# Running a feed-forward stage inside the steps of a state-space stage, block by block

## Chip, cores and metric

The kernel runs on one core of a Trainium2 chip. The metric is the device time of one execution in microseconds, as the median of several. The engines are TensorE (PE, with its weight loads PEld), VectorE (DVE), ScalarE (ACT), GpSimd (POOL) and SyncE (SP), which here only issues DMAs. Each engine works through its own queue in the order in which the program writes it, and waits on semaphores for the others.

## What is computed

Four layers follow each other over x of 16 sequences x 256 tokens x 128 channels. A windowed attention, a mixture-of-experts layer with an attention of its own, a state-space layer (third stage) and a gated MLP (last stage). Only the last two matter here. In the reference's terms, for the third:

```python
xn = layernorm(x); u, z = split(xn @ W_in)
u = silu(causal_depthwise_conv(u, conv_w) + conv_b)
dt = softplus(u @ dt_w + dt_b); Bm, Cm = u @ B_w, u @ C_w
h_t = h_{t-1} * exp(dt_t * A) + (dt_t * u_t) Bm_t;  y_t = h_t . Cm_t
x = x + layernorm(x_n + ((y + u * D) * silu(z)) @ W_out)
```

and for the last, token by token, with ternary weights and scales s:

```python
xn = layernorm(x)
hid = silu(xn @ w1 * s1) * (xn @ w2 * s2)      # 512 wide, gate and up
hid = gelu(hid @ h1 * t1); hid = gelu(hid @ h2 * t2)
x = x + layernorm(hid @ w3 * s3)
```

## The kernel before

**Tiling.** The channels or the tokens lie on 128 partitions. The third stage takes one sequence of 256 tokens per step; the state is handed from chunk to chunk of 8 tokens, and from one half of a sequence to the next. The last stage takes blocks of 512 tokens (two sequences), two blocks ("lanes") per pass, four passes. x stays in SBUF as xB. The precise matmuls split each operand into a high and a low part (`product`, L1405): three matmuls, high x high, low x high, high x low. A hidden product of the last stage has four groups (m), each of four k blocks x 3 matmuls of 128x512; a gate product has two times three. The last product takes sixteen 128x128 matmuls in float32.

**Order.** All is written out by hand. Each engine has a function `step_c(n, have)` for the third stage, called for n = 0 to 18, which holds that engine's share of work on sequences n-3 to n+4: a software pipeline. `have(k)` says whether sequence n+k exists. After it comes `step_d` for the last stage, called for the four passes. The loops stand at the end of each engine's part, for TensorE as

```python
pairs(0)
for n in range(0, NB + 3):
    step_c(n, within(n))
    if n == NB - 1:
        step_d(-1, 0, within(-1, ITER_MLP))
for n in range(0, ITER_MLP + 1):
    step_d(n, 0, within(n, ITER_MLP))
```

`step_d(-1)` norms and turns the first two blocks inside step 15.

**A step of the third stage.** TensorE: B and C inputs (`in_and_out`), step size (`step_size`), turning the next input (`turned_input`), outputs from states (`from_states`), C by chunk (`outputs_by_chunk`), the convolution as four shifted matmuls and z's matmul (`convolved`), the chunks' weights turned (`chunk_weights`), B by chunk (`inputs_by_chunk`), states (`chunk_states`), output product (`projected`), products of token pairs (`pairs`), turned states (`turned_states`). VectorE (L1300): the conv input, seven decay products (L1194), from states (L1203), terms (L1215, L1218: decay x pair products), adding (L1227), dt (L1239), masked C (L1244), gating (L1233), the scan (L1248), statistics, weighted input, states (L1270 to L1278), residual, masked B (L1288), the output norm's statistics. ScalarE (L852): Relu and Abs of dt (L764), the input turned (L781), Exp and Ln, skip path, `normed`, Silu of u and z (L812), two Exp for the decays (L818), output norm, states out, and B and C (L759). Its functions lie in different tables: Ln, Silu and Exp each load theirs, three loads a step. GpSimd: the pair sums (L546, L548), small norm arithmetic, products, and adding to xB (L560).

**A block of the last stage.** `gate` is Silu of the gate product (L901), `hid` the up product times scale and gate (L1347, "raised" in the change), h_h its high part (L892) and h_l its low part (L1340). Gelu after hidden product 1 is L909, with high part L910, and after hidden product 2 L914. The last product (L1843) is scaled on VectorE (L1374), normed (L109, L112, L118, L119, L141), added on GpSimd (L594) and stored by SyncE (L425).

**Buffers.** PSUM has eight banks. The third stage uses 0 to 3 for input, dt/C, B and state, 4 to 7 for the four groups of pair products, and 7 (2 for sequence 0) also for B and C. The last stage uses four banks per lane. The last stage's buffers lie over the third's in SBUF. The weights' high parts are made on ScalarE (L881, L884) and their low parts on GpSimd (L506), a quarter in step 14, the rest in the steps after 15.

## Time and profile before

| | |
|---|---|
| median of three runs | 1014.7 us |
| lowest and highest | 1014.23, 1015.83 us |
| profiled execution | 1014.94 us |
| its span | 1013.1 us |
| TensorE, VectorE, ScalarE, GpSimd busy | 84%, 67%, 55%, 44% |
| mean granted clock of TensorE | 0.85 |

The rows that follow come from one profiled execution. A row of a timeline gives start in us, duration in us, engine, line and operation, output <- input, shapes and count, and in brackets how long the engine had been idle and who released it. A window gives the busy time of each engine in a stretch. The granted clock is 1.00 at 2.4 GHz and 0.50 at 1.2 GHz; a value between is a mean over time. The stretch from about 500 to 720 us is the third stage, that from 731 us on the last.

### The profile page before, as it was taken

The numbers are of one execution on the slowest core, as the hardware profiler recorded it, in microseconds if no ns is written. First come the engines' busy times: TensorE is split into PE (matmuls) and PEld (weight loads), VectorE is DVE, ScalarE is ACT, GpSimd is POOL, SyncE is SP. The second block draws the span as 40 slices with busy tenths as digits, with TensorE's granted clock in tenths as the row PEclk, the third lists the DMA queues.
The fourth block names the chain that finished last, engine by engine and source line by source line (L and its number), as shares of the span: only waits on it lengthen the run. The fifth ranks groups of instructions, "written<-read, shape, count | busy, mean of one in ns | idle before, by whom it ended". The sixth has DMA issues, their size and how long they took to land. (4 is left out here: it accounts for less than half of the span.)

```text
span 1013.1 us, 21506 instructions
## 1 busy us (share of the span) xinstructions
PE 849.9 (84%) x8256; PEld 700.1 (69%) x8256; DVE 678.9 (67%) x1965; ACT 555.2 (55%) x1050; POOL 448.3 (44%) x765
## 2 busy tenths in 40 slices
PE   4887836789999999898587798887579999999994
PEld 4777735678888888676455576655468878888783
DVE  3888954757888878742499999999772180551712
ACT  3454523347666666546477877877354362542630
POOL 1676752314555554544477777866650020020201
PEclk9877865559999989887788977788589999999997
DMA  8300002000000000000000000000000000000000
GB/s 273 101 24 12 24 27 65 17 1 2 2 2 2 2 3 2 1 2 1 1 1 0 1 1 1 2 1 0 1 1 1 1 21 1 1 22 1 16 6 21
DMA packets 22149, 16.76 MB, mean 17 GB/s; under 512 B 2576, under 2 KB 20376, under 8 KB 21792
## 3 DMA queue, kind: packets, MB, share of 16 engines
q1 hardware_dynamic: 21040, 14.77, 4.7%
q8 instruction: 65, 1.06, 0.4%
q10 hardware_dynamic: 1008, 0.63, 0.2%
q14 instruction: 36, 0.29, 0.1%
HBM read 11.20 MB, written 4.19 MB: 15 GB/s over the span
## 5 line engine op out<-in xcount | busy, mean ns | idle before, releaser
L118 POOL TENSOR_TENSOR d_ln_ve<-d_ln_mv,eps 128x4 f32<-128x4 f32 x16 | 3.2, 201 | 228.3 <-DVE d_ln_mv L112 228.3
L1408 PE MATMUL ps<-h_h,wh_l 128*128 128x512 f32 x256 | 99.6, 389 | 0.0
L1409 PE MATMUL ps<-h_l,wh_h 128*128 128x512 f32 x256 | 99.6, 389 | 0.0
L1407 PE MATMUL ps<-h_h,wh_h 128*128 128x512 f32 x256 | 99.6, 389 | 0.0
L1486 PE MATMUL ps<-w_e,he 128*128 128x128 f32 x512 | 87.4, 310 | 3.7 <-ACT he L679 3.3
L679 ACT ACTIVATE he<-ps,pp 128x256 f32<-128x256 f32 x128 | 59.6, 471 | 43.9 <-PE ps L1409 39.2
L1486 PEld LDWEIGHTS ps<-w_e,he 128*128 128x128 f32 x512 | 77.2, 222 | 6.1 <-ACT he L679 5.4
L1420 PEld LDWEIGHTS ps<-mov,hbd 32*128 32x128 f32 x2048 | 75.1, 224 | 0.0
L1374 DVE TENSOR_TENSOR d_y<-ps,w_s 128x512 f32<-128x512 f32 x8 | 5.5, 692 | 103.0 <-PE ps L1843 103.0
L1420 PE MATMUL ps<-mov,hbd 32*128 32x32 f32 (+1 forms) x2048 | 74.0, 300 | 0.0
L1340 DVE TENSOR_TENSOR h_l<-hid,h_h 128x512 fp32r<-128x512 f32 x64 | 48.5, 772 | 31.2 <-ACT h_h L910 30.3
L118 POOL TENSOR_TENSOR b_ln_ve<-b_ln_mv,eps 128x2 f32<-128x2 f32 x64 | 13.1, 204 | 111.4 <-DVE b_ln_mv L112 111.4
L914 ACT ACTIVATE hid<-ps,pp 128x512 f32<-128x512 f32 x32 | 22.1, 690 | 62.3 <-PE ps L1409 62.3
L1407 PEld LDWEIGHTS ps<-h_h,wh_h 128*128 128x128 f32 x256 | 48.1, 188 | 10.1
L1409 PEld LDWEIGHTS ps<-h_l,wh_h 128*128 128x128 f32 x256 | 48.1, 188 | 10.0
L1408 PEld LDWEIGHTS ps<-h_h,wh_l 128*128 128x128 f32 x256 | 48.1, 188 | 9.9
L653 ACT ACTIVATE tau<-ps 128x768 f32<-128x768 f32 x32 | 24.2, 809 | 55.6 <-PE ps L1420 55.6
L1407 PE MATMUL ps<-hTh,we_h 128*128 128x256 f32 x128 | 53.6, 419 | 0.0
L1194 DVE TENSOR_TENSOR wall<-dec,wall 128x224 f32<-128x224 f32 (+6 forms) x112 | 47.8, 427 | 3.7 <-issue 0.3
L546 POOL TENSOR_TENSOR term<-term 128x224 f32<-128x224 f32 (+2 forms) x48 | 35.4, 737 | 32.4 <-DVE term L1218 29.9
L119 POOL TENSOR_TENSOR b_ln_rs<-b_ln_ve,half 128x2 f32<-128x2 f32 x64 | 46.0, 718 | 5.0
L1764 PE MATMUL ps<-ident,hc 128*128 128x128 f32 x64 | 15.0, 371 | 37.9 <-DVE hc L1278 37.9
(287 smaller groups left out, 2597.8 us busy)
## 6 DMA issues: line engine op xcount, KB each, us to landing
x<-in_x SPq DMA_DIRECT2D x16, 128.0 KB
w_h<-in_w_h SPq DMA_DIRECT2D x2, 1024.0 KB, 7.9
x<-x SPq DMA_DIRECT2D x16, 128.0 KB, 1.8
xB<-x SPq DMA_DIRECT2D x32, 64.0 KB
out_x<-xB SPq DMA_DIRECT2D x32, 64.0 KB
w_m<-in_w_m SPq DMA_DIRECT2D x3, 256.0 KB, 3.8
xB<-in_w_e SPq DMA_DIRECT2D x1, 512.0 KB
w_e<-in_w_e SPq DMA_DIRECT2D x1, 512.0 KB
```

The lines of the kernel that those rows point to most:

```text
L119: pool.tensor_tensor(self.rs[l][:, :], self.ve[l][:, :], half[:, 0:self.k], ALU.pow).then_inc(self.rstd_ready, 1)
L546: chain.link(pool.tensor_tensor(y[:, :, j:CH], y[:, :, j:CH], wide[:, HALF - 1 - j, :, j:CH], ALU.add))
L653: act.activation(tau[l][:, 2 * k:2 * k + 2, :], ps[:, 4 * l + 2 * k:4 * l + 2 * k + 2, 0:NBLK * SPAN], ACT.Sigmoid, scale=ATT_SCALE).then_ ...
L679: act.activation(he[e % 2][:, :], ps[:, HE + e % 2, 0:NT], ACT.Gelu, bias=vec("b1", e)).then_inc(he_ready, 1)
L914: act.activation(hid[l][:, m, :], bank(l, m), ACT.Gelu, scale=vec("h2_s", m)).then_inc(m_h2, 1)
L1194: ins = dve.tensor_tensor(wall[l][:, :, CH - 1 - j, j:CH], dec[l][:, 0, :, j:CH], wall[l][:, :, CH - j, j - 1:CH - 1], ALU.mult)
L1340: dve.tensor_tensor(dst[l][:, m, :], hid[l][:, m, :], high_part[l][:, m, :].bitcast(F32), ALU.subtract).then_inc(done, 1)
L1407: pe.matmul(dst, a_h, b_h, start=start, stop=True, skip_group_check=True)
L1408: pe.matmul(dst, a_l, b_h, start=False, stop=True, skip_group_check=True)
L1409: return pe.matmul(dst, a_h, b_l, start=False, stop=True, skip_group_check=True)
L1420: return pe.matmul(dst, hbd[l][heads(g), j, :, :].rearrange("p h s -> p (h s)"), mov[l][heads(g), BLK * j:BLK * j + w], start=False, stop= ...
L1486: last = pe.matmul(ps[:, ACC, P * c:P * c + P], he[e % 2][:, P * c:P * c + P], w_e2[:, e, :], start=False, stop=True, skip_group_check=True)
```

## The change

Blocks of 512 tokens of the last stage run inside the third stage's steps. Let b be a block: sequences 2b and 2b+1. In step n = 2b+4 ("entering") its tokens are normed and turned and gate products 0 and 1 are made; in step 2b+5 ("middle") gate products 2 and 3 and hidden product 1; in step 2b+6 ("ending") hidden product 2 and the last product; in step 2b+7 ("leaving") the output norm and the addition to xB. So an odd step has a middle block, an even one an ending and an entering one. The steps now run from 0 to 16 only. What is left after step 16, the rest of block 6 and all of block 7 but its place in memory, stands in a `tail()` on each engine, with PSUM banks of its own (`TAIL_UP`, `TAIL_HIDDEN`).

To make room, the last stage has one lane: a single `hid`, `h0`, `h1`, `d_xn`, `d_xh`, `d_y` and two `gate` and two `raw` buffers, some of them over the raw weights' memory. In PSUM the pair products get two banks (4, 5) and are made in two halves, `pairs(t, 0)` and `pairs(t, 1)`, with `terms` in two halves as well; the second half of `pairs` stands behind the convolution. Banks 6 and 7 are the last stage's; its last product goes to bank 2. The weights are split in ten parts, two in each of steps 0 to 4. The output norm of the third stage writes in place and comes a step earlier. TensorE's new `step_c`, cut:

```diff
             def step_c(n, have):
+                entering, middle, ending = block_of(n, 4), block_of(n, 5), block_of(n, 6)
                 if have(1):
                     in_and_out(n + 1)
                     step_size(n + 1)
...
                     from_states(n - 1)
+                if ending is not None:
+                    hidden(ending, 1, 0)
                 if have(1):
                     outputs_by_chunk(n + 1)
+                if middle is not None:
+                    gate_and_up(middle, 2)
                 if have(2):
                     convolved(n + 2)
+                if middle is not None:
+                    if have(1):
+                        inputs_by_chunk(n + 1)
+                    gate_and_up(middle, 3)
+                if have(0):
+                    pairs(n, 1)
+                if ending is not None:
+                    hidden(ending, 1, 1)
                 if have(0):
                     chunk_weights(n)
-                if have(1):
+                if middle is None and have(1):
                     inputs_by_chunk(n + 1)
+                if ending is not None:
+                    hidden(ending, 1, 2)
                 if have(0):
                     chunk_states(n)
+                if middle is not None:
+                    if have(1):
+                        pairs(n + 1, 0)
+                    hidden(middle, 0, 0)
                 if have(-1):
                     projected(n - 1)
-                if have(1):
-                    pairs(n + 1)
+                if ending is not None:
+                    hidden(ending, 1, 3)
+                if entering is not None:
+                    tokens_turned(entering)
+                if middle is None and have(1):
+                    pairs(n + 1, 0)
+                if middle is not None:
+                    hidden(middle, 0, 1)
                 if have(0):
                     turned_states(n)
+                if middle is not None:
+                    hidden(middle, 0, 2)
+                    hidden(middle, 0, 3)
+                if entering is not None:
+                    gate_and_up(entering, 0)
+                if ending is not None:
+                    last_product(ending)
+                if entering is not None:
+                    gate_and_up(entering, 1)
```

The new functions on TensorE, with what they wait for:

```diff
+            def gate_and_up(b, m):
+                if m == 0:
...
+                    pe.wait_ge(S["d_xl"], b + 1)
...
+                elif b < LAST - 1 or b == LAST - 1 and m == 1:
+
+                    pe.wait_ge(m_raw, nth(b, m - 1))
...
+            def hidden(b, w, m):
+                src_h, src_l, ready, done = ((h0_h, h0_l, m_h0, m_h1_ps), (h1_h, h1_l, m_h1, m_h2_ps))[w]
+                if m == 0:
...
+                    pe.wait_ge(ready, nth(b, HID - 1))
+                elif m >= 2 and b < LAST - 1:
+
+                    pe.wait_ge((m_h1_high, m_h2)[w], nth(b, m - 2))
```

ScalarE's and VectorE's new `step_c`, as the order of their calls (what is new stands with its block):

```diff
             def step_c(n, have):          # ScalarE
...
                     log_part(n + 1)
                 if have(0):
                     skip_path(n)
+                if middle is not None:
+                    high0(middle, 1)
+                    gated(middle, 2)
+                if ending is not None:
+                    hidden2(ending, 0)
                 if have(2):
                     normed(n + 2)
+                if ending is not None:
+                    hidden2(ending, 1)
+                if middle is None and have(0):
                     chunk_weights(n)
+                if ending is not None:
+                    hidden2(ending, 2)
+                    hidden2(ending, 3)
+                if entering is not None:
+                    turned_tokens(entering)
                 if have(2):
                     silus(n + 2)
+                if middle is not None:
+                    high0(middle, 2)
+                    gated(middle, 3)
+                    if have(0):
+                        chunk_weights(n)
+                    high0(middle, 3)
+                if entering is not None:
+                    gated(entering, 0)
...
+                    gated(entering, 1)
                 if have(1):
                     decays(n + 1)
+                if entering is not None:
+                    high0(entering, 0)
+                if middle is not None:
+                    hidden1(middle, 0)
...
             def step_c(n, have):          # VectorE
+                if entering is not None:
+                    tokens_in(entering)
                 if have(2):
                     conv_input(n + 2)
+                if leaving is not None:
+                    tokens_out(leaving)
+                if middle is not None:
+                    raised(middle, 1)
+                if ending is not None:
+                    low1(ending, 2)
+                    low1(ending, 3)
                 if have(0):
                     decay_products(n)
                 if have(-1):
                     from_states(n - 1)
+                if middle is not None:
+                    low0(middle, 0)
+                    low0(middle, 1)
+                    raised(middle, 2)
+                if have(0):
+                    terms(n, 0)
+                if have(1):
+                    step_size(n + 1)
+                if entering is not None:
+                    tokens_normed(entering)
+                if have(1):
+                    outputs_by_chunk(n + 1)
+                if middle is not None:
+                    low0(middle, 2)
+                    if have(1):
+                        summed_steps(n + 1)
+                    raised(middle, 3)
+                if have(0):
+                    terms(n, 1)
+                if middle is not None:
+                    low0(middle, 3)
...
                 if have(-1):
                     add_sums(n - 1)
                     gated(n - 1)
                 if have(1):
                     weighted_input(n + 1)
+                if leaving is not None:
+                    output_normed(leaving)
...
+                if entering is not None:
+                    tokens_low(entering)
                 if have(4):
                     statistics(n + 4)
+                if entering is not None:
+                    raised(entering, 0)
...
+                if ending is not None:
+                    scaled(ending)
+                if middle is not None:
+                    low1(middle, 0)
+                    low1(middle, 1)
```

In the last of these, `raised` is the up product times scale and gate into `raw`, `low0` and `low1` are low parts, `scaled` is the scaling of the last product, `tokens_in` and `tokens_out` are statistics, `tokens_normed` and `output_normed` apply norms. On ScalarE `high0` is the copy to the high part, `hidden1` Gelu with its copy, `hidden2` Gelu alone. SyncE's loop over the blocks is written out, with the same four stores a block.

## Rows read from the trace of the kernel before

**Rows 1.** The page: busy time of each engine; TensorE's granted clock in 40 slices.

```profile
PE 849.9 (84%) x8256; PEld 700.1 (69%) x8256; DVE 678.9 (67%) x1965; ACT 555.2 (55%) x1050; POOL 448.3 (44%) x765
...
PEclk9877865559999989887788977788589999999997
```

**Rows 2.** Windows: stretch, busy PE, PEld, DVE, ACT, POOL (x), clock, DMA.

```profile
550.00:600.00 50.00, 39.56 (x242) 29.34 (x240) 47.59 (x117) 39.00 (x80) 38.43 (x78) 0.82 0.00 1
...
800.00:850.00 50.00, 48.49 (x234) 40.14 (x233) 28.83 (x76) 26.35 (x39) 7.30 (x10) 1.00 0.04 11
```

**Rows 3.** One line: min/median/max ns, first, last start; one per step.

```profile
L1276 DVE TENSOR_TENSOR hc<-hd,ps x16: 420/420/422, 512.4 to 718.2; 128x256 f32<-128x256 f32 x16
```

**Rows 4.** Timeline, VectorE, last stage: start, duration, engine, line, [idle <-releaser].

```profile
800.35 0.69 DVE L1374 TENSOR_TENSOR d_y<-ps,w_s 128x512 f32<-128x512 f32 x1 [23.32 <-PE ps L1843]
...
994.66 0.69 DVE L1374 TENSOR_TENSOR d_y<-ps,w_s 128x512 f32<-128x512 f32 x1 [23.32 <-PE ps L1843]
```

**Rows 5.** Timeline, TensorE, third stage: one step.

```profile
596.88 0.75 PE L1764 MATMUL ps<-ident,hc 128*128 128x128 f32 x4 [1.28 <-DVE hc L1278]
...
606.62 0.93 PE L1757 MATMUL ps<-prod,ones 32*128 32x384 f32 x8
```

**Rows 6.** Timeline, TensorE, last stage: gate, hidden and last products.

```profile
816.35 0.40 PE L1407 MATMUL ps<-d_xh,wm_h 128*128 128x512 f32 x1
...
817.74 0.39 PE L1407 MATMUL ps<-h_h,wh_h 128*128 128x512 f32 x1
...
820.46 0.39 PE L1407 MATMUL ps<-h_h,wh_h 128*128 128x512 f32 x1
...
990.82 7.30 PE L1843 MATMUL ps<-w_m,hid 128*128 128x128 f32 x64
```

**Rows 7.** Timeline, ScalarE, third stage; the last row is Exp between Gelu calls.

```profile
595.07 1.28 ACT L818 ACT_TABLE_LOAD   x1
...
597.18 0.86 ACT L133 ACTIVATE c_o<-c_r,c_ln_nm,c_ln_rs 128x128 f32<-128x128 f32 x2
...
598.89 0.47 ACT L764 ACTIVATE c_zb<-ps,pp 128x256 f32<-128x256 f32 x1 [0.21 <-PE ps L1678]
...
602.95 0.86 ACT L798 ACTIVATE c_xn<-xB,c_ln_nm,c_rs 128x128 f32<-128x128 f32 x2
...
460.27 1.28 ACT L716 ACT_TABLE_LOAD   x1
```

**Rows 8.** Timeline, VectorE, third stage.

```profile
616.12 1.21 DVE L1215 TENSOR_TENSOR term<-wall,ps 128x1024 f32<-128x1024 f32 x1
...
617.85 0.41 DVE L1227 TENSOR_TENSOR c_yi<-c_yi,term 128x256 f32<-128x256 f32 x1
...
620.83 0.46 DVE L109 BATCH_NORM_STATS2 c_ln_st<-xB 128x6 f32<-128x128 f32 x2
```

**Rows 9.** Timeline, VectorE and ScalarE, last stage: element-wise operations.

```profile
817.28 0.75 DVE L1347 SCALAR_TENSOR_TENSOR hid<-ps,pp,gate 128x512 f32<-128x512 f32 x1 [1.10 <-ACT gate L901]
...
815.49 0.69 DVE L1340 TENSOR_TENSOR h_l<-hid,h_h 128x512 fp32r<-128x512 f32 x1
...
816.55 0.69 ACT L901 ACTIVATE gate<-ps,pp 128x512 f32<-128x512 f32 x1 [1.10 <-PE ps L1409]
...
832.27 0.63 ACT L910 ACTIVATE h_h<-hid 128x512 fp32r<-128x512 f32 x1
```

**Rows 10.** Windows, TensorE alone: one that is mostly idle, and the next.

```profile
524.58:528.00 3.42, 0.54 (x3) 0.90 0.00 0
...
528.00:531.41 3.41, 3.41 (x31) 0.60 0.03 7
```

**Rows 11.** One line: low parts of the last weights, GpSimd.

```profile
L506 POOL TENSOR_TENSOR wm_l<-w_m,wm_h x2: 1314/1338/1361, 709.7 to 711.0; 128x512 fp32r<-128x512 f32 x2
```

**Rows 12.** Timeline, TensorE, start of the last stage.

```profile
748.50 0.50 PE L1407 MATMUL ps<-d_xh,wm_h 128*128 128x512 f32 x1 [3.42 <-DVE hid L1347]
```

**Rows 13.** Timeline, end of the kernel: VectorE's scaling.

```profile
998.26 0.69 DVE L1374 TENSOR_TENSOR d_y<-ps,w_s 128x512 f32<-128x512 f32 x1 [2.91 <-PE ps L1843]
```

531 lines of the change are left out of this document (313 added, 218 removed).

## Prediction

> **What bounds the kernel now.** I read the page first. TensorE is busy 84% of the span, VectorE 67%, ScalarE 55%, and the granted clock is lowest where the third stage runs [rows 1]. A share over the whole span says little here, so the windows come next. They show two regimes. In the third stage VectorE is busy 47.6 of 50 us and TensorE 39.6 at a granted clock of 0.82; in the last stage TensorE is busy 48.5 of 50 us at 1.00, and VectorE only 28.8 [rows 2]. So the third stage hangs on VectorE's queue, the last on TensorE's, and work of the one could lie in the other's gaps. The rates: 16 steps of the third stage start one per (718.2 - 512.4)/15 = 13.72 us [rows 3]; three passes of the last stage take 994.66 - 800.35 = 194.3 us, 64.8 us for two blocks, 32.4 a block [rows 4]. Two steps and one block, which the change puts together, thus cost 27.4 + 32.4 = 59.8 us now.
>
> **What two steps and a block cost TensorE.** One step's operations run from 596.88 to 607.55, 10.7 us [rows 5], part of it at the half clock; at full clock I take 9.6. A gate product is 817.74 - 816.35 = 1.4 us, a group of a hidden product 820.46 - 817.74 = 2.72, the last products 7.30/2 = 3.6 [rows 6], turning the tokens 0.4 (estimate, four matmuls at 7.30/64). A block is 4 x 1.4 + 8 x 2.72 + 3.6 + 0.4 = 31.4. With two steps that is 50.6 us against 59.8. That is the least the pair can take, and 9 us of gain per pair the most.
>
> **What the order leaves of it.** The queues are written out by hand, so I walk them. An odd step has gate products 2 and 3 and hidden product 1 of the middle block, an even one hidden product 2 and the last products of the ending block and the first two gate products of the entering one. Time zero is the end of the even step's last products.
>
> (a) TensorE makes gate product 1, 1.4. ScalarE then has in its queue Silu 0.7 (and 0.14 to be released), a table load with two Exp, 597.18 - 595.07 = 2.1, a copy to the high part 0.6, the copy of bcT 0.3, then step size, turned input, Exp, table load, Ln and skip path, 602.95 - 598.89 = 4.1, a copy 0.6, and a table load with Silu 2.0: gate 2 is there at 11.8 [rows 6, 7, 9]. TensorE waits for parts of this: for the step size's Relu and Abs (about 1.7 us), and with gate product 3 for the raised gate 2 (about 1.8).
>
> (b) VectorE now has raised gate 2, both halves of terms, step size, masked outputs, the scan, two low parts and raised gate 3 ahead of the last low part of the hidden input. From terms to the scan's end it is 620.83 - 616.12 = 4.7, less 0.9 for adding and gating, which stay behind (the first takes 0.41), plus 0.1 for splitting terms in two; raised gates 0.75 and low parts 0.69 each, two of either: 6.7 us in all [rows 8, 9]. GpSimd waits for terms at that time, so that I take 0.6 off for operations that run longer beside it. Only then, at 18, may hidden product 1 begin. TensorE had waited another 2.2 us.
>
> (c) Four hidden groups 10.9, output product and turned states 1.2: 12.1. VectorE keeps ahead.
>
> (d) The even step on TensorE: 9.6 + 10.9 + 0.4 + 1.4 + 3.6 = 25.9, and 0.5 of waiting for the token's low part. ScalarE has five table loads there but reaches all of its releases in time by my walk, and VectorE has some 20 us of work in 27.
>
> The pair is 11.8 + 6.7 - 0.6 + 12.1 + 26.4 = 56.4 us.
>
> **The clock.** A mostly idle stretch (0.54 of 3.42 us busy) is followed by a slow phase of about 3.4 us, at 0.5, in all: 0.10 and 0.40 of two rows' clock is missing, twice that is the slow time [rows 10]. It costs 1.7 us if TensorE is what is waited for, nothing in front of a wait. The odd step's waits of 1.7, 1.8 and 2.2 us lie beside small matmuls, and before this change a wait of 1.28 us at 596 [rows 5] stood in a stretch with clock 0.82 [rows 2]. Bounds: 0, and 5.4 (three slow phases of which one falls on gate product 3, one on the first hidden group and one on the even step's first). I take one, 1.8: the first is absorbed by the wait after it. The pair is then 58.2 us, 1.6 under that of before.
>
> **The edits with a small price.** Pair products in two halves: the second half now stands behind the convolution, and it waits for the first half's terms. In steps 0 to 4 VectorE comes to the second half of terms about when TensorE has done the convolution at full clock, and up to 2 us earlier at half clock: bounds 0.1 and 2, I take 1.0 for five steps, 5.0. The weights' split goes from the boundary into steps 0 to 4. GpSimd gets 2 x 1.34 us a step [rows 11] on 10.5 of 13.7 (38.4 of 50 [rows 2]); it just fits (bounds 0 and 0.5 a step, in the 5.0). ScalarE gets 2 x 0.6; the last pair delays step 5 by 1.3. More table loads: 3 a pair, since Gelu comes into the steps and Exp after Gelu needs one, as in the second stage [rows 7]; they are in the walk. Output norm a step earlier and in place, the residual's wait for c_x, the shared bank of the last products: their releasers are over two steps old, nothing. SyncE's stores: the same four per block, earlier, under other work; the final ones have the same length behind them. Single buffers (raw, gate, d_y, banks 6 and 7): each wait's releaser comes in time by the walk, except those counted.
>
> **The sum**, in the profiled execution's own time. VectorE enters step 4 at about 556 (567.3 by rows 3, less the 11.5 us that stand ahead of that line in the step, estimate). Step 4 takes 13.9 and the tokens' statistics, norm, low part 3.0, plus gate product, Silu and raised gate behind it, less what covers them, 1.6: 574.2. With 5.0 and 1.3: 580.5. Five pairs 291.0: 871.5. Step 15 has no input to prepare: (a) shrinks to 8, 8 + 6.5 - 0.6 + 12.1 + 1.6 = 27.6: 899.1. Step 16: from states 1.6, hidden product 10.9, gate 1.4, last 3.6, small ones 1.0, waits 2.7: 21.2: 920.3. The tail: 1.4 gate product and 7.0 of waiting for gates 2 and 3 and their low parts; hidden groups 4 x 10.9; gates 5.6; last 7.2; turning with its wait 1.1; waits of 2.2 and 0.9 in front of the last block's two final products, which no second lane covers any more; end 12.7 (1013.1 - 998.3 [rows 13] and 0.2, less one block's norm, 2.3); one slow phase 1.7 and 0.6 more: 84.0. **The span is 1004.3.** What pays most is not the pair (5 x 1.6 = 8) but the boundary: its first pass, with waits as long as 3.42 us [rows 12], and the 10 us in which neither stage fed TensorE are gone, some 15 us, of which steps 0 to 4 and the tail take back about 14. The execution took 1014.94 for a span of 1013.1, 1.8 more, and lies 0.2 over the median 1014.7 of three runs: 1004.3 + 1.8 = 1006.1, so **1006**.
>
> **Rivals.** *The odd step is a chain, and TensorE runs it at half clock* (slower). Place: gate product 2, convolution, gate product 3 and the first hidden group, behind the waits of (a) and (b). Price: 3.6 more per pair, the upper bound 5.4 less 1.8: 5.5 x 3.6 = 20, 1026. It decides from 1.6 us more per pair on, where the pair costs what it costs now. For it: clock 0.82 in the third stage; in-order queues of which three engines have 20 to 24 us of work in one odd step. Against it: hidden groups are dense, and the clock was 1.00 in the last stage. Chance 0.27. *No loss by the clock*: 56.4 a pair, 10 us less, 996; chance 0.17. *The order hides nearly everything*, the pair near 51 to 53: 1006 - 5.5 x 6 = 973, chance 0.10. It needs ScalarE to reach gate 2 some 4 us earlier than the durations add up to. *The stages don't overlap but alternate*: nothing but the boundary is gained and lost, within 2 us of now; 0.07. Mine, 997 to 1012: 0.39.
>
> ScalarE's switches of table could be dearer than I took them. Here a load and two Exp take 2.11 us from start to start [rows 7], which is 1.28 and two times 0.42. The Trainium skill, "ScalarE: Activation LUTs", What ACT_TABLE_LOAD costs, gives each switch a drain of about 1.38 us beside the load's 1.28. By that rule, three switches in (a) would add 4.1 us to every pair and 23 to the sum, 1029, on the slow side. The trace shows no room for the drain, so that I give it next to nothing.
>
> **How the numbers follow.** A run of this kernel can be told from no change at about 0.2%, 2 us. Faster takes mine, no clock loss and full hiding, 0.66; same 0.07; slower 0.27. The range leaves out most of full hiding and the slow rival's far end: 982 to 1030.
>
> **What would show it.** Starts of L1276's successor: odd plus even step 58 us, the odd 29 or more. TensorE's waits inside the odd step for the raised gate and for the hidden low part, each near 2 us. Clock 0.85 to 0.95 between 575 and 900. VectorE and ScalarE each busy 70 to 80% there. The tail from about 920. I am wrong if the odd step's waits are short, if the even step has waits over 2 us, or if steps 0 to 4 take over 15.5 us.

## The result and the profile after

The changed kernel takes 1027.56 us (median of 4 runs, 1023.85 to 1028.78) against 1014.7 us: ratio 1.0119, 95% interval 1.0092 to 1.0146. The forecast was 1006 and "faster"; the kernel is slower. On a second chip it took 1028.78 us, ratio 1.0103 (1.0038 to 1.0168). Ratios here and below leave out the few executions that fell in the chip's slower state, so that some differ a little from the quotient of the medians.

First the page of the changed kernel: busy time by engine, and the granted clock in 40 slices. The busy shares look like those of before [rows 1]: TensorE 84% in both. The clock differs in three places: it is lower in slices 2 to 4, which lie in the first stage (7, 6, 6 against 8, 7, 7), lower in slices 20 to 24, the third stage's first steps (6, 8, 7, 7, 7 against 7, 8, 8, 9, 7), and higher in slices 25 to 29, where the two stages now run together (all 9 against 7, 7, 8, 8, 5).

```profile
span 1025.6 us, 21514 instructions
PE 858.2 (84%) x8256; PEld 694.7 (68%) x8256; DVE 681.8 (66%) x1997; ACT 573.3 (56%) x1072; POOL 446.5 (44%) x771
PEclk9766865559999999887687779999999999999898
```

The windows separate the stretches (columns: stretch, its length, then busy time and count of TensorE, its weight loads, VectorE, ScalarE, GpSimd, the clock, DMA share and GB/s). From 520.3 to 571 are steps 1 to 3, to 600 step 4 and the first gate products, from 700 on full pairs.

```profile
520.30:571.00 50.70, 38.78 (x198) 27.88 (x198) 42.67 (x99) 35.42 (x70) 36.23 (x65) 0.80 0.00 1
571.00:600.00 29.00, 18.27 (x81) 12.97 (x81) 19.53 (x55) 11.45 (x24) 16.26 (x33) 0.64 0.00 1
700.00:750.00 50.00, 44.79 (x251) 34.65 (x250) 34.78 (x90) 31.15 (x56) 19.93 (x38) 1.00 0.00 1
```

In this stretch of the pairs TensorE is busy 45 of 50 us at full clock, where the third stage alone had 39.6 at 0.82 [rows 2]. There the change does what it says. In steps 1 to 4 no engine is full: VectorE is busy 42.7 of 50.7 us and then 19.5 of 29, where it had 47.6 of 50 [rows 2].

**Marks for the comparison.** The last write of `he` ends the second stage, the last one of `hc` ends VectorE's share of a step's recurrence, and `d_y` is scaled when a block's last products are done. The rows of the changed kernel (the one of `he` gives min, median and max in ns, first and last start and shapes; the others are rows of the timeline):

```profile
L719 ACT ACTIVATE he<-ps,pp x128: 448/473/478, 216.4 to 498.2; 128x256 f32<-128x256 f32 x128
520.29 0.42 DVE L1376 TENSOR_TENSOR hc<-hd,ps 128x256 f32<-128x256 f32 x1
536.16 0.42 DVE L1376 TENSOR_TENSOR hc<-hd,ps 128x256 f32<-128x256 f32 x1
553.65 0.42 DVE L1376 TENSOR_TENSOR hc<-hd,ps 128x256 f32<-128x256 f32 x1
570.76 0.42 DVE L1376 TENSOR_TENSOR hc<-hd,ps 128x256 f32<-128x256 f32 x1
594.15 0.42 DVE L1376 TENSOR_TENSOR hc<-hd,ps 128x256 f32<-128x256 f32 x1
L1440 DVE TENSOR_TENSOR d_y<-ps,w_s x8: 691/692/692, 659.4 to 1015.1; 128x512 f32<-128x512 f32 x8
```

Steps 1 to 4 are 15.9, 17.5, 17.1 and 23.4 us long, each from one last write of `hc` to the next. Before, three steps took 552.88 - 512.37 = 40.5 us, 13.5 each, and step 4 13.9 (by the first write of `hc`, L1276, of which [rows 3] has the first and the last row).

The last `he` starts at 494.4 us before and at 498.2 after, although the code up to there is the same. Over the kernels of this study, all alike up to there, that mark lies between 490.2 and 504.9 us. It goes with TensorE's clock in the first stage: over the first 130 us the granted clock was 0.86 before, 0.80 in the changed kernel, and 0.76 in its second profile, whose mark is the one at 504.9. So I compare what follows it: 1013.1 - 494.4 = 518.7 us before, 1025.6 - 498.2 = 527.4 after, and 527.5 in the second profile of the changed kernel. **The part that was changed lost 8.7 us.** The other 3.8 of this pair of profiles lie ahead of the mark. I take them for scatter of the early stages; with one profile of the kernel before that is not shown, and the medians (12.9 us apart here, by the interval 9.3 to 14.8, and 10.5 by the ratio on the second chip) leave room for a small loss there too.

### The profile page after: what moved, and what is told of

It reads as the page before. It is cut to its first block, busy times and chain, and to the rows that moved or that the text cites. A ratio compares the mean times of both kernels' runs of the same rounds, so it can differ in the third digit from the quotient of the medians.

```text
span 1025.6 us, 21514 instructions
## 1 busy us (share of the span) xinstructions
PE 858.2 (84%) x8256; PEld 694.7 (68%) x8256; DVE 681.8 (66%) x1997; ACT 573.3 (56%) x1072; POOL 446.5 (44%) x771
## 4 chain that ended last, share of the span: by engine, by line
PE 65%; DVE 17%; ACT 8%; issue 5%; POOL 3%; DMA 1%; ACTq 0%; POOLq 0%; SPq 0%; DVEq 0%
PE ps L1580 12%; PE ps L1582 9%; PE ps L1581 9%; PE ps L1659 6%; PE ps L1593 6%; PE ps L1881 3%; PE ps L1999 3%; PE ps L1652 2%; PE ps L1575 2%; PE ps L1599 2%; PE ps L1935 1%; DVE vbd L1047 1%; PE ps L1941 1%; PE ps L1683 1%; DVE a_ln_st L108 1%
## 5 line engine op out<-in xcount | busy, mean ns | idle before, releaser
L1580 PE MATMUL ps<-h_h,wh_h 128*128 128x512 f32 x256 | 106.4, 416 | 10.6 <-DVE h_l L1429 6.5
L1582 PE MATMUL ps<-h_l,wh_h 128*128 128x512 f32 x256 | 101.7, 397 | 0.0
L1593 PEld LDWEIGHTS ps<-mov,hbd 32*128 32x128 f32 x2048 | 78.5, 233 | 0.0
L1593 PE MATMUL ps<-mov,hbd 32*128 32x32 f32 (+1 forms) x2048 | 77.4, 308 | 0.0
L577 POOL TENSOR_TENSOR term<-term 128x224 f32<-128x224 f32 (+2 forms) x48 | 38.9, 811 | 84.2 <-DVE term L1316 81.7
L1582 PEld LDWEIGHTS ps<-h_l,wh_h 128*128 128x128 f32 x256 | 48.9, 191 | 11.1
L1421 DVE SCALAR_TENSOR_TENSOR raw<-ps,pp,gate 128x512 f32<-128x512 f32 x32 | 23.7, 744 | 43.1 <-ACT gate L905 42.7
L919 ACT ACTIVATE raw<-ps,pp 128x512 f32<-128x512 f32 x32 | 22.0, 688 | 49.4 <-PE ps L1582 49.4
L925 ACT ACTIVATE hid<-ps,pp 128x512 f32<-128x512 f32 x24 | 16.5, 688 | 52.6 <-PE ps L1582 52.5
L1652 PE MATMUL ps<-hotTb,negsel 8*128 8x256 bf16 x128 | 37.7, 294 | 9.0 <-ACT he L719 6.9
L905 ACT ACTIVATE gate<-ps,pp 128x512 f32<-128x512 f32 x32 | 21.7, 686 | 35.0 <-PE ps L1582 34.9
```

The lines of the kernel that those rows point to most:

```text
L577: chain.link(pool.tensor_tensor(y[:, :, j:CH], y[:, :, j:CH], wide[:, HALF - 1 - j, :, j:CH], ALU.add))
L1580: pe.matmul(dst, a_h, b_h, start=start, stop=True, skip_group_check=True)
L1582: return pe.matmul(dst, a_h, b_l, start=False, stop=True, skip_group_check=True)
L1593: return pe.matmul(dst, hbd[l][heads(g), j, :, :].rearrange("p h s -> p (h s)"), mov[l][heads(g), BLK * j:BLK * j + w], start=False, stop= ...
L1652: pe.matmul(bk, negsel[:, e, :], hotTb[q % 2][:, :], start=True, stop=True, skip_group_check=True)
```

## The experiments

For each kernel: the median, the ratio to the kernel before on the same chip, and from its profile the time from the last `he` to the first `d_y` (steps 0 to 6) and to the end. The kernel before took 1016.61, 1014.68, 1022.31 and 1014.97 us on the chips of the four groups (r0, e1, e3, e4; e2, e5, e6, e7; e8, e9; e10), so that ratios, not medians, compare across groups. The last two columns come from one profile each. The time to the first `d_y` repeats well: 161.2 and 161.3 us in the changed kernel's two profiles, 147.7 to 147.8 in four kernels that differ little up to there. The stretch behind it took 365.4 to 367.3 us in kernels with the same code there, so that a difference of 1 or 2 us in the last column alone says nothing.

| kernel | median us | ratio, 95% interval | to first d_y | to the end |
|---|---|---|---|---|
| before | 1014.7 | | | 518.7 |
| changed | 1027.56 | 1.0119 (1.0092 to 1.0146) | 161.2 | 527.4 |
| changed, other chip | 1028.78 | 1.0103 (1.0038 to 1.0168) | 161.3 | 527.5 |
| e1, whole pair products, steps 0 to 4 | 1009.79 | 0.9937 (0.9903 to 0.9970) | 147.7 | 513.9 |
| e2, halves ahead of the convolution | 1023.51 | 1.0086 (1.0052 to 1.0120) | 156.5 | 521.9 |
| e8, as e2, banks of their own | 1021.52 | 0.9976 (0.9927 to 1.0025) | 151.3 | 518.6 |
| e3, tokens taken in later | 1026.80 | 1.0114 (1.0078 to 1.0150) | 157.8 | 530.7 |
| e4, ScalarE: gate 2 first | 1035.39 | 1.0174 (1.0105 to 1.0243) | 164.8 | 538.0 |
| e5, e1 and tokens later in step 4 | 1007.47 | 0.9936 (0.9906 to 0.9965) | 147.7 | 513.9 |
| e6, e5 and heads' weight earlier | 1009.15 | 0.9935 (0.9914 to 0.9955) | 147.8 | 513.8 |
| e7, e6 and gates earlier | 1006.61 | 0.9914 (0.9884 to 0.9944) | 147.7 | 510.7 |
| e9, e7 and step size later | 1017.96 | 0.9957 (0.9917 to 0.9998) | 149.1 | 513.6 |
| e10, e6 without the weights' low parts | 1008.92 | 0.9935 (0.9902 to 0.9967) | 144.7 | 511.8 |

**The changed kernel once more, beside the first experiments.**

> The changed kernel again, as the reference beside the experiments. Expected 1024 to 1029 us. What is open: in its first trace the first stage, which the change doesn't touch, ended 4 us later than before (last Sigmoid at 139.2 against 134.9 us). If memory placement is the cause the same row stands at 139 again; if it is the state of TensorE's clock, it moves between runs by some us, to either side.

It came out at 1028.78 us with the same steps, 15.9, 17.5, 17.3 and 23.3 us. The last Sigmoid started at 144.5 us, not at 139 again, in a profile whose clock there was lower still: it moves between runs, with the clock.

### What the second half of the pair products costs

These rows of TensorE are step 2 of the changed kernel (start, duration, shapes and count, and in brackets the idle time before and who ended it):

```profile
542.29 3.12 PE L1881 MATMUL ps<-c_xT,w_conv 128*128 128x256 f32 x8
...
545.78 0.92 PE L1935 MATMUL ps<-prod,ones 32*128 32x384 f32 x4
554.13 0.75 PE L1941 MATMUL ps<-ident,hc 128*128 128x128 f32 x4 [2.46 <-DVE hc L1376]
```

and this is what VectorE waited for from step 0 to the end of step 4's terms (in all, times, longest), its three largest:

```profile
DVE term L1313 <- PE ps L1935: 8.9, 4, 2.6
DVE d_ln_st L108 <- POOL xB L591: 3.1, 1, 3.1
DVE c_dt L1337 <- ACT c_sp L811: 1.5, 2, 1.1
```

Two things stand in them. VectorE waits 8.9 us for the second half, 1.9 to 2.6 us in steps 0, 2, 3 and 4 and not at all in step 1, and the second half stands behind a convolution of 3.12 us; the pace maker of these steps now waits for TensorE. And half of the pair products, four records, takes 0.92 us, as long as all eight took before, 0.93 [rows 5]. So I undid the split in steps 0 to 4, where the four banks are free anyway:

```
+        WHOLE = 5
...
-                for g in range(2):
+                for g in range(4 if t < WHOLE else 2):
```

with the second call and VectorE's second reading left out there.

> One part undone: for sequences 0 to 4 the four pair products are made together again, in banks 4 to 7, and terms in one piece. Theory A: the second half of the pair products, which stands behind the convolution, has put TensorE's convolution into the loop of steps 0 to 4. Then their periods (15.9, 17.5, 17.1 us for steps 1 to 3) fall to 13.8 to 14.2, and the whole to 1014 to 1018 us. Rival B: the weights' split, now in these steps (1.1 us on ScalarE ahead of the step size, 2.5 us on GpSimd), makes them long. Then the periods stay above 16 and the gain is under 4 us.

1009.79 us, ratio 0.9937. Steps 1 to 4 are 14.3, 14.5, 15.2 and 20.9 us, and the time to the end falls by 13.5 us, all of it in front of the first `d_y`. The wait for the pair products is gone, and the convolution in step 2 takes 2.06 us:

```profile
533.36 2.06 PE L1887 MATMUL ps<-c_xT,w_conv 128*128 128x256 f32 x8
538.67 0.93 PE L1943 MATMUL ps<-prod,ones 32*128 32x384 f32 x8
```

**One edit turns the change from slower to 0.6% faster than before.** TensorE had the same matmuls from the last `he` to the first `d_y` (629 and 630 in the two windows) and was busy with them for 115.3 us in place of 125.3, at a granted clock of 0.86 in place of 0.82. Is it the place or the split? In e2 the halves stay, both ahead of the convolution:

```
+                if n < 5:
+                    pairs(n, 1)
                 if middle is not None:
                     gate_and_up(middle, 2)
                 if have(2):
                     convolved(n + 2)
...
-                if have(0):
+                if have(0) and n >= 5:
                     pairs(n, 1)
```

> The changed kernel, but in the third stage's steps both halves of the pair products stand ahead of the convolution again (still as two halves). Placement theory: the second half behind the convolution is what VectorE waited for in steps 0 to 4 (8.9 us in 4 waits); with it ahead, the steps 1 to 3, 15.9, 17.5 and 17.1 us long in the changed kernel, fall to 14.5 to 15.5 us, and the whole to 1016 to 1020 us; it stays a little above the kernel with whole pair products, since two halves cost TensorE some 0.9 us more than one piece. Rival, the halving itself: steps 1 to 3 stay above 15.9 us and the whole gains under 4 us.

Steps 1 to 4 are 15.5, 16.9, 17.1 and 21.4 us. Against my placement theory, only 4.7 of the 13.5 us come back, and the ratio (1.0086 against 1.0119 and 1.0103) does not tell the two kernels apart. Step 2 of e2 on TensorE:

```profile
539.02 1.65 PE L1935 MATMUL ps<-prod,ones 32*128 32x384 f32 x4 [0.50 <-DVE term L1316]
540.60 3.78 PE L1881 MATMUL ps<-c_xT,w_conv 128*128 128x256 f32 x8
```

The second half uses the banks of the first, so it waits until VectorE has read them. TensorE was at half clock already, from its wait of 2.46 us for `hc` at 532.67 on, and it stays there for the second half and the convolution: 1.65 and 3.78 us. e8 gives each half banks of its own in steps 0 to 4:

```
+        own = lambda t, k: PAIRS + (2 * k if t < 5 else 0)
...
-                    last = pe.matmul(ps[:, PAIRS + g, 0:BC_AT], ones[part, :], prod[l][part, :], start=True, stop=True)
+                    last = pe.matmul(ps[:, own(t, k) + g, 0:BC_AT], ones[part, :], prod[l][part, :], start=True, stop=True)
```

> Both halves of the pair products ahead of the convolution, as in the run with the placement alone undone, but in steps 0 to 4 each half has banks of its own, so that the second does not wait until VectorE has read the first. Theory that the halving costs through that wait (0.50 us of idle in step 1 there, and behind it the second half and the convolution at half clock, 1.65 and 3.78 us in place of 0.91 and 2.06): steps 1 to 3, 15.5, 16.9 and 17.1 us there, fall to within 0.5 us of the 14.3, 14.5 and 15.2 us of the whole products, and the profiled execution to about 1010 us. Rival, the time of two halves itself (0.9 us more on TensorE each step) and VectorE's later second term: steps 1 to 3 stay above 15.4 us on the mean and the profiled execution above 1013 us.

```profile
534.81 0.91 PE L1936 MATMUL ps<-prod,ones 32*128 32x384 f32 x4
535.65 2.01 PE L1882 MATMUL ps<-c_xT,w_conv 128*128 128x256 f32 x8
```

The same place in e8: the wait is gone, and the clock is back up at the second half and the convolution. Steps 1 to 3 are 15.3, 15.5 and 16.8 us: the mean is 15.9, so the rival (over 15.4) was right that the two pieces cost by themselves. On the chip of e8 the ratio to the kernel before (0.9976, 0.9927 to 1.0025) shows no difference either way. Over the same 50 us, 513 to 563, the granted clock tells the order, first e1, then e2, then e8:

```profile
513.00:563.00 50.00, 35.10 (x220) 26.02 (x220) 45.10 (x109) 39.40 (x79) 39.36 (x75) 0.84 0.00 1
513.00:563.00 50.00, 40.48 (x201) 28.46 (x200) 41.98 (x97) 34.77 (x70) 35.52 (x64) 0.75 0.00 1
513.00:563.00 50.00, 39.26 (x222) 27.71 (x218) 43.72 (x107) 37.72 (x75) 36.56 (x68) 0.80 0.00 1
```

e2's TensorE is busy 5.4 us longer than e1's for fewer matmuls, as its lower clock would have it. To the first `d_y` the ladder is 161.2 (changed), 156.5 (both ahead), 151.3 (own banks), 147.7 (whole): 3.6 us are what two pieces cost even without a wait for a bank. That is near the 0.9 us that each of five steps pays on TensorE, but the clock is lower too (0.84 in e8 and 0.86 in e1, from the last `he` to the first `d_y`), and the runs don't part the two. Of the other 9.9, 4.7 go with the place and 5.2 more with banks of their own. Halves with banks of their own behind the convolution were not run, so that this division holds for this order of the two edits.

### Step 4

Step 4 takes in the tokens of the first block. VectorE's, TensorE's and GpSimd's rows there in the changed kernel:

```profile
574.90 0.72 POOL L591 TENSOR_TENSOR xB<-xB,c_r 128x256 f32<-128x256 f32 x1
575.65 0.87 DVE L108 BATCH_NORM_STATS2 d_ln_st<-xB 128x6 f32<-128x128 f32 x4 [3.14 <-POOL xB L591]
579.35 0.66 PE L1575 MATMUL ps<-ident,c_xq 128*128 128x128 f32 x2 [5.56 <-DVE c_xq L1281]
```

VectorE waits for GpSimd's addition to `xB`, and the convolution's input stands behind that in its queue, so TensorE is idle 5.56 us. e3 takes the tokens in behind the decay products, in every step:

```
-                if entering is not None:
-                    tokens_in(entering)
                 if have(2):
                     conv_input(n + 2)
...
                 if have(0):
                     decay_products(n)
+                if entering is not None:
+                    tokens_in(entering)
```

> One order changed on VectorE: the entering block's statistics stand behind the decay products and no longer ahead of the conv input. Theory C: they wait for GpSimd's addition (3.1 us in step 4, 2.2 in later even steps) and hold the conv input and with it TensorE's turned input (5.6 us idle in step 4) and the clock. Then step 4 becomes 3 to 5 us shorter and the whole 4 to 8 us. Rival D: the next wait takes its place, pair products in step 4 and TensorE's full queue in the others: under 2 us in all.

Step 4 falls from 23.4 to 19.9 us, but the four pairs that follow the first `d_y` grow from 231.6 to 236.2 us, and the end comes 3.3 us later than in the changed kernel, so that the theory was right on step 4 alone (3 to 5 us) and not on the whole. In these four pairs TensorE's clock is 0.96 in e3 and 0.99 in the changed kernel, and TensorE waits 4.6 us for VectorE's terms in place of 1.6, while its 4.5 us of waits for the raised gate are gone. Why the clock is lower there was not followed further. So e5, on top of e1, does it in step 4 alone.

> The kernel with whole pair products ahead of the convolution (1009.8 us), and in step 4 alone the tokens of the next step are taken in behind the decay products, so that VectorE's statistics don't wait for GpSimd's addition (3.14 us at 575.65 in the changed kernel) ahead of what TensorE needs. Theory that step 4 is a stretch of its own in which that wait holds the convolution: step 4, 20.9 us there, falls to about 17.5 us and the whole by 3 to 3.5 us, to about 1006 us. Rival, another wait (gate 0's chain on ScalarE and VectorE) is as late: under 1 us.

Step 4 falls by 1.9 us (20.9 to 19.0) and step 5 grows by 2.1 (29.8 to 31.9); to the first `d_y` it is 147.7 us in both. The rival held, in that nothing is gained. These are rows of e5, the last two the first records of gate products 0 and 1:

```profile
566.47 2.51 DVE L140 TENSOR_SCALAR d_xn<-xB,d_ln_mv,d_ln_rs 128x128 f32<-128x128 f32 x4 [2.10 <-POOL d_ln_rs L118]
575.42 0.77 PE L1588 MATMUL ps<-d_xh,wm_h 128*128 128x512 f32 x1
579.89 0.80 PE L1588 MATMUL ps<-d_xh,wm_h 128*128 128x512 f32 x1 [1.56 <-DVE raw L1427]
```

against these of e1:

```profile
579.09 0.77 PE L1586 MATMUL ps<-d_xh,wm_h 128*128 128x512 f32 x1
583.38 0.50 PE L1586 MATMUL ps<-d_xh,wm_h 128*128 128x512 f32 x1 [1.56 <-DVE raw L1427]
```

The norm now waits 2.10 us for GpSimd's root. Gate product 1 still begins earlier, 87.8 us behind the last `he` in place of 89.5, but from there to the first `d_y` it takes 59.9 us at a clock of 0.92 in place of 58.2 at 0.97. In both kernels the clock had fallen ahead of gate product 0 (0.77 us for its first record); in e1 it rose again within the wait of 1.56 us, and in e5 only behind gate product 1. So the 1.7 us that were won are given back by the clock.

### The other work in steps 0 to 4

e6 moves ScalarE's split of the weights by a few operations, ahead of the states' copy:

```
+                if n < 4:
+                    weight_heads(n)
                 if entering is None and have(0):
                     states_out(n)
```

> As the run with step 4 changed, and in steps 0 to 3 ScalarE's weight of the heads (1.14 us) stands ahead of the states' copies. Theory that ScalarE's order holds VectorE in these steps (1.08 us at 527.53, 0.47 us at 543.41): steps 1 to 3 fall from 14.3, 14.5 and 15.2 us to 13.9 to 14.2 us, the whole by 1 to 2 us. Rival: the wait is hidden or another takes its place, no difference.

Nothing moved: 14.3, 14.5 and 15.2 us again, 147.8 to the first `d_y`. VectorE's 1.5 us of waits for `c_sp` in the changed kernel are down to 0.1 in e1 already (L1343, its step size), so there was nothing left to gain. That leaves GpSimd's side of the split. e10 takes it out:

```
-                pool.tensor_tensor(lo, w, hi.bitcast(F32), ALU.subtract).then_inc(m_low, 1)
+                pool.memset(lo.bitcast(F32), 0.0).then_inc(m_low, 1)
```

> The run with the heads' weight moved, but GpSimd sets the low parts of the last stage's weights to zero in place of computing them (two a step, 1.27 us each, in steps 0 to 4), so that the output lacks their share. Theory that these subtractions, new in steps 0 to 4, lengthen VectorE's operations that run beside them (decay products 456 ns in place of 406, gating 1015 in place of 588, weighted input 752 in place of 452): steps 1 to 3, 14.3, 14.5 and 15.2 us long in that run, fall to 13.5 to 13.9 us as before the change, and the time from the last output of the second stage to the end by 3 to 5 us. Rival, the step's new order alone makes it longer: steps 1 to 3 stay within 0.3 us of 14.3, 14.5 and 15.2.

Steps 1 to 4 are 13.7, 14.2, 14.7 and 17.4 us, 43.9 to 42.7 for the first three and 1.5 less for step 4; the first `d_y` comes 3.1 us earlier. That is the theory's direction, but only step 1 falls into its range, the end comes 2.0 us earlier where 3 to 5 had been expected, and the ratio (0.9935 for both) shows no gain of the whole. The groups of VectorE over steps 1 to 3 (busy time, mean ns of one, idle before), first e6, then e10, whose row of L1294 is the same as e6's:

```profile
L1294 DVE TENSOR_TENSOR wall<-dec,wall 128x224 f32<-128x224 f32 (+6 forms) x21 | 9.6, 456 | 0.8 <-ACT dec L860 0.2
L1339 DVE TENSOR_TENSOR c_ya<-c_yi,c_zs 128x256 f32<-128x256 f32 x3 | 3.0, 1015 | 0.1
L1345 DVE SCALAR_TENSOR_TENSOR c_dt<-c_sp,c_zb 128x256 f32<-128x256 f32 x3 | 2.8, 936 | 0.1
L1333 DVE TENSOR_TENSOR c_yi<-c_yi,term 128x256 f32<-128x256 f32 x3 | 1.6, 539 | 0.0
```

```profile
L1339 DVE TENSOR_TENSOR c_ya<-c_yi,c_zs 128x256 f32<-128x256 f32 x3 | 2.5, 849 | 0.1
L1345 DVE SCALAR_TENSOR_TENSOR c_dt<-c_sp,c_zb 128x256 f32<-128x256 f32 x3 | 1.2, 416 | 0.1
L1333 DVE TENSOR_TENSOR c_yi<-c_yi,term 128x256 f32<-128x256 f32 x3 | 2.4, 790 | 0.0
```

Step size (936 to 416 ns) and gating (1015 to 849) get faster without GpSimd's subtractions beside them, as do two more operations (752 to 630 and 939 to 841 ns), 0.91 us a step in all. But the first addition of the terms gets slower (539 to 790 ns), and the scan as well (687 to 911): 0.48 us a step go back. In e10 all three additions have GpSimd's pair sums (L578) beside them and take 0.79 us; in e6 the one that has them takes 0.79 as well, and the two beside small operations of GpSimd 0.41 and 0.42. What is left, 0.43 us, is what a step got shorter on the mean. The decay products stay at 456 ns, where they took 406 before, so their 0.35 us a step (7 times 50 ns) is not the subtractions'. The memsets still take 0.52 us each, so 3.1 us is what 0.75 us less for each of ten pieces gives. What none of GpSimd's share would give was not run.

### What holds a pair of steps

In the changed kernel the odd step between two `d_y` looks like this on TensorE, from gate product 1 to the first hidden group:

```profile
717.67 0.48 PE L1580 MATMUL ps<-d_xh,wm_h 128*128 128x512 f32 x1
723.69 0.70 PE L1871 MATMUL ps<-c_xs,w_cR 128*128 128x256 f32 x2 [2.35 <-ACT c_sp L805]
730.32 0.50 PE L1580 MATMUL ps<-d_xh,wm_h 128*128 128x512 f32 x1 [1.50 <-DVE raw L1421]
733.80 1.10 PE L1912 MATMUL ps<-bbd,wendT 128*128 128x256 f32 x4 [0.56 <-ACT wendT L844]
735.74 0.50 PE L1580 MATMUL ps<-h_h,wh_h 128*128 128x512 f32 x1
```

All three waits lead to ScalarE's queue, the second by way of VectorE, whose raised gate 2 waits for ScalarE's Silu. e4 changes its order, gate 2 ahead of the step size's Exp and Ln, and the decays ahead of gate 1:

```
+                if middle is not None:
+                    high0(middle, 1)
+                    gated(middle, 2)
                 if have(1):
                     log_part(n + 1)
                 if have(0):
                     skip_path(n)
-                if middle is not None:
-                    high0(middle, 1)
-                    gated(middle, 2)
...
+                    if have(1):
+                        decays(n + 1)
                     gated(entering, 1)
-                if have(1):
-                    decays(n + 1)
```

> Order changed on ScalarE alone, with two more table loads a pair: decays ahead of gate 1 in even steps, gate 2 ahead of Exp and Ln in odd ones. Theory E: the odd step is set by ScalarE's chain to gate 2. Then odd steps become 2 to 3.5 us shorter, a pair 54.5 to 56 in place of 57.8, the whole 1011 to 1018 us. Rival F: VectorE's own queue in the odd step sets it: a pair stays within 0.7 us of 57.8. Rival G: the two loads are paid: a pair of 58.5 or more.

The pairs take 59.1 to 61.2 us in place of 57.3 to 58.6. That is the range of rival G. Gate 2 does come earlier, 6.5 us behind gate product 1 in place of 11.1 (725.95 - 719.49 against 728.79 - 717.67), but gate 3, whose product was done at 730.3, waits in ScalarE's queue until 733.74, behind what used to stand ahead of gate 2, with the table loads of that. Rows of ScalarE, then of TensorE:

```profile
726.66 1.28 ACT L810 ACT_TABLE_LOAD   x1
727.95 0.42 ACT L810 ACTIVATE c_sp<-c_sp 128x256 f32<-128x256 f32 x1
728.38 1.28 ACT L811 ACT_TABLE_LOAD   x1
...
733.74 0.69 ACT L905 ACTIVATE gate<-ps,pp 128x512 f32<-128x512 f32 x1
734.84 2.04 PE L1914 MATMUL ps<-bbd,wendT 128*128 128x256 f32 x4 [3.23 <-ACT wendT L844]
738.47 0.80 PE L1582 MATMUL ps<-h_h,wh_h 128*128 128x512 f32 x1
```

TensorE is idle 3.23 us for the copy behind the gate, and the work behind it, the hidden group too, runs at half clock. e7, on top of e6 and of e4's order, moves gate 3 and the high parts up too:

```
                 if have(1):
                     log_part(n + 1)
+                if middle is not None:
+                    high0(middle, 2)
+                    gated(middle, 3)
+                    if have(0):
+                        chunk_weights(n)
                 if have(0):
                     skip_path(n)
...
+                if middle is not None:
+                    high0(middle, 3)
                 if have(2):
                     silus(n + 2)
-                if middle is not None:
-                    high0(middle, 2)
-                    gated(middle, 3)
-                    if have(0):
-                        chunk_weights(n)
-                    high0(middle, 3)
```

> As the run before it, and ScalarE's order in the steps of a block is changed: the decays ahead of gate 1 in even steps, and in odd steps the gated parts 1 to 3 between the step's own parts, each as soon as its product is done. Theory that the pair of steps (57.8 us) is a ring through ScalarE's queue: the first hidden product starts 15.5 us behind the last products of the step before in place of 17.9, the pair falls to about 55.5 us and the whole by about 13 us, to 992 to 996 us. Rival, a new wait in ScalarE's queue and a half-clocked TensorE behind it, as where gate 2 alone was moved: the pair stays at 57.8 us or above.

The four pairs take 57.7, 56.1, 57.3 and 57.0 us, 3.4 us less over the four than in e1, and the end comes 3.2 us earlier; 13 had been expected. 1006.61 us is the fastest median here, though its interval (0.9884 to 0.9944) overlaps that of e1. TensorE's rows in e7:

```profile
764.96 1.64 PE L1925 MATMUL ps<-bbd,wendT 128*128 128x256 f32 x4 [1.43 <-ACT wendT L845]
768.12 0.80 PE L1593 MATMUL ps<-h_h,wh_h 128*128 128x512 f32 x1
```

The first hidden group begins 768.12 - 751.42 = 16.7 us behind gate product 1, against 18.07 in the changed kernel, but behind 1.43 us of idling it and the products ahead of it run at half clock: 1.4 us are won at the start, and the clock takes some of them back: from the first hidden group to the next gate product 1 it is 40.6 us, where the changed kernel has 39.8. e9 fills that wait. On TensorE, in odd steps:

```
                     gate_and_up(middle, 2)
-                if have(2):
-                    convolved(n + 2)
-                if middle is not None:
                     if have(1):
                         inputs_by_chunk(n + 1)
                     gate_and_up(middle, 3)
+                    if have(0):
+                        chunk_weights(n)
+                if have(2):
+                    convolved(n + 2)
...
-                if have(0):
+                if middle is None and have(0):
                     chunk_weights(n)
```

with ScalarE's Exp and Ln of the step size behind gate 3 and its high part, and VectorE's step size behind the last low part, the summing and the gating.

> The kernel with the gates moved on ScalarE, and in odd steps the third gate product and the turned chunk weights stand ahead of the convolution on TensorE, gates 2 and 3 and the last high part ahead of the step size's Exp and Ln on ScalarE, and VectorE's step size behind the last low part. Theory that a pair of steps there (57.3 us) is held by TensorE's idle 1.43 us for ScalarE's copy of the chunk weights and by the half clock behind it (3.0 us of nine hidden products at 0.63 in place of 0.39 us spacing 0.43 to 0.23, the rest on the matmuls ahead): the pair falls to 54 to 55 us and the whole by 12 to 18 us, to 989 to 995 us. Rival, the step size, 3 to 5 us later now, holds the decays, the states and the next step: the pair stays at 57 us or above, with TensorE waiting elsewhere.

The pairs take 56.7, 58.2, 58.2 and 57.8 us, not 54 to 55; the end is 2.9 us later than in e7. The rival (57 or above) held in three of the four. TensorE's rows in e9:

```profile
774.38 0.50 PE L1592 MATMUL ps<-d_xh,wm_h 128*128 128x512 f32 x1 [1.33 <-DVE raw L1430]
781.34 0.50 PE L1592 MATMUL ps<-h_h,wh_h 128*128 128x512 f32 x1
789.16 0.75 PE L1956 MATMUL ps<-ident,hc 128*128 128x128 f32 x4 [1.60 <-DVE hc L1385]
```

The first hidden group now begins 15.6 us behind gate product 1 (765.77), and at full clock. But the states `hc` are there only 23.4 us behind it, so that TensorE, which comes earlier, waits 1.60 us for them in the middle of hidden product 1, and the groups behind run at half clock again. From the first hidden group to the next gate product 1 it is 42.7 us in place of 39.8. Four orders of the queues (changed, e4, e7, e9) gave pairs of 56.1 to 61.2 us; where one wait of TensorE got shorter, another one or the half clock showed.

## Why the prediction was wrong

**Right: the pair, for partly the wrong reason.** Forecast 58.2, measured 57.3 to 58.6; five pairs, from gate product 1 to gate product 1, forecast 291.0, measured 890.68 - 599.88 = 290.8. The first hidden group was forecast at 17.9 and came at 735.74 - 717.67 = 18.07 us. The three waits were forecast as 1.7, 1.8 and 2.2 and came as 2.35, 1.50 and 0.56, and the third is another one than I had: 2.2 was for VectorE's last low part, for which TensorE doesn't wait here, and 0.56 is for ScalarE's copy of the chunk weights. The clock term is where I was lucky: I took 1.8 us for it, but the clock was 1.00 in the last three of the five pairs (57.3 to 57.9 us); in the first two it was 0.95 and 0.94, and they took 59.2 and 58.6. The walk was short by 1.3 us elsewhere: from the first hidden group to the next gate product 1 it has 38.5 us, the trace some 39.8.

**Right: the end.** Steps 15 and 16 forecast 48.8, measured 939.40 - 890.68 = 48.7; the tail forecast 84.0, measured 1025.6 - 939.4 = 86.2.

**Right: ScalarE's table loads.** A rule of the Trainium skill ("ScalarE: Activation LUTs", What ACT_TABLE_LOAD costs) would have added a drain to each switch, and 23 us to the sum. In e4's rows the Exp starts 1.29 us behind its load's start and the next load at once behind the Exp: no drain. By the pairs' length, too, the trace disagrees with the rule here: 57.3 to 58.6 us, where 58.2 had been forecast without drains and 62.3 would be the sum with them.

**Wrong: everything ahead of the first pair.** I had gate product 1 of the first block at 580.5, that is 86.1 us behind the last `he`; it came at 599.88 - 498.2 = 101.7. These 15.6 us and the tail's 2.2, less the 0.3 by which the pairs and steps 15 and 16 came out shorter, are the 17.5 that the changed part missed (527.4 against 1004.3 - 494.4 = 509.9); the stages ahead of the mark gave 3.8 more. The step that failed is this one: "up to 2 us earlier at half clock: bounds 0.1 and 2, I take 1.0 for five steps, 5.0". The mechanism was named, but its size was wrong: the halves' price is 13.5 us (changed to e1), 2.7 a step in place of 1.0 and above the upper bound of 2. Of it 12.2 lie ahead of gate product 1 (101.7 against 89.5) and 1.3 behind it. Three things stand behind it. (1) Two halves cost 0.9 us a step more on TensorE, for which the prediction has no term. (2) The second half stands behind the convolution, and once VectorE waits for it, TensorE too has gaps; the clock over steps 1 to 3 is 0.80, where it was 0.90 before (512.4 to 562.4), and a convolution of 3.12 us in place of 2.06 is then in the loop. I had kept that for the upper bound. (3) VectorE's wait for the second half was 2.2 us on the mean where it came, in four steps of five: 8.9 us in all, against the 5.0 that I took for everything. How the 13.5 us divide among the three is shown only as far as e2 and e8 go.

With whole pair products the part ahead of gate product 1 is still 89.5 us (583.38 - 493.9), against 81.1 forecast without the 5.0. Of these 8.4 us, steps 1 to 3 show 44.0 - 40.5 = 3.5 and the rest lies in step 4. GpSimd's subtractions, which I had called just fitting at up to 0.5 us a step, hold at least 3.0 of it (gate product 1 in e6 and e10: 87.8 and 84.8 us behind the last `he`). For step 4 I had left out that the tokens' statistics wait for GpSimd's addition, 3.14 us, with the convolution's input queued behind them. Taken away (e5), it brings gate product 1 forward by 1.7 us and nothing to the end, since the clock takes them back. The rest of the 8.4 is 3.7 us: 2.2 in steps 1 to 3 (42.7 in e10 against 40.5 before), with the longer decay products among them, and some 1.5 in step 4. How they divide further is open.

**The rivals.** The one that ended on the slow side was the right sign with the wrong place: it put 20 us of half clock into the pairs, which ran at 0.94 to 1.00, while the loss stood in steps 0 to 4. Its 1026 is near the 1027.56 measured by luck. The last sentence of the prediction had the condition that was met, "if steps 0 to 4 take over 15.5 us". Had the halves cost the 5.0 that I took, the end would lie at about 519 us behind the last `he`, which is no change; with none of it, at 513.9, it is e1, 0.6% faster than before. My sum had 509.9 with the 5.0 in it: 9 us too low even if that term had been right, and 1006 was too good.

## What to carry to other kernels

When a piece of work is split, look up in a row what half of it costs, and when it is moved behind something else on an in-order queue, ask who waits for it at each place of the loop, not only in the stretch for which it was moved. Here the split and the late place were made for the steps that share banks with the last stage, and 13.5 us were paid for them in the five steps that don't; what they cost in the others was not measured. A wait in such a loop can be paid twice, as itself and in TensorE's clock behind it; a reordering that shortens a chain is worth only what is left when the next wait's clock is counted.

## What the runs showed of the hardware

- Four records of 32x384 take 0.91 to 0.92 us at full clock, and eight, in one sequence, 0.93. In e1's trace the eight start four at a time (538.67 to 538.69 and 539.10 to 539.12 us), in the changed kernel two at a time, 0.43 us apart as well (545.78 and 546.21): the groups, which use different 32 rows each, run beside one another, and half of them saves nothing.
- Whether TensorE ran at 1.2 GHz behind a wait did not follow the wait's length. Behind 1.43 us (e7) and 3.23 us (e4) the hidden group began with a record of 0.80 us, where the records ahead of the wait had been at full clock; behind 2.35 us in the changed kernel the gate product's records had 0.39. And in e1 the clock rose within a wait of 1.56 us, where it stayed at half in e5. It has to be read for each place.
- VectorE's step size took 936 ns in e6 and 416 in e10, with only GpSimd's subtractions exchanged for memsets, while the first addition of the terms took 539 and 790: in these two runs it is 0.41 to 0.42 us beside small operations of GpSimd and 0.79 beside its pair sums. L1319, which reads PSUM, took 1205 in both.
- A GpSimd subtraction of 128x512 took 1.27 us, a memset of the same size 0.52.
